# One ScalarE operation for both 16-bit planes of a tile, in place of one on ScalarE and one on GpSimd

## The chip, the cores and the metric

The kernel runs on one core of one Trainium2 chip. The metric is the device time of one execution in microseconds, from the first to the last instruction and a little around them; lower is better. The engines are named as the profile names them: PE is TensorE (PEld its weight loads), DVE is VectorE, ACT is ScalarE, POOL is GpSimd and SP is SyncE, which here only issues DMAs.

## The reference

One block of a network on 1024 tokens of width 512: a layer norm, then a Mamba-2 mixer and a mixture-of-experts linear layer on its output, both added to the input. What matters here is the mixer:

```python
xn = _layernorm(x)
proj = einsum('bsd,ed->bse', xn, in_proj_w)          # gate | hBC | dt
hBC = silu(causal_conv4(hBC) + conv_b)               # depthwise, 4 taps
hs, Bm, Cm = split(hBC)                              # hs: 128 heads of 64
...                                                  # chunks of 128 tokens:
Y = Y_diag + Y_off + hs * D                          # scan with decays exp(cumsum(dt * A))
g = Y * silu(gate)
out = groupwise_rms_norm(g) * norm_w
return x + einsum('bsi,oi->bso', out, out_proj_w) + moe(xn)
```

All of it is in fp32. The kernel keeps that precision by splitting operands of matmuls into a high and a low part (names that end in H and L), so a product takes three matmuls.

## The kernel before

The mixer is cut into 16 slices of 8 heads and each slice into 8 chunks of 128 tokens. The main loop runs over the 128 pairs, here called steps m = 0 to 127, with s = m // 8 the slice and c = m % 8 the chunk. Every engine has its own program, an order written out by hand, and engines meet only at semaphores. Each engine takes its instructions strictly in order.

In a step TensorE does, in this order: blocks of the B/C tile (L324, L325), a part of the input projection of a later slice (L257 to L259), the two state products (L446 to L458), 32 small products of the decay matrix EM (L466), the output projection of the step before (L476 to L483), the gate product of the next step (L334 to L341), and last the transposes of the gated result yb (L491). The result yb is made by VectorE: L1045 adds the parts of Y in PSUM and L1048 multiplies by the gate. So L1048 of step m must end before L491 of step m can start.

The tiles that feed the slices are [128 channels, 1024 tokens]. Such a tile passes through: projection on TensorE (into two PSUM banks), `act_tap` on ScalarE (L516, first tap of the convolution), `dve_conv` on VectorE (L784, three more taps, one after the other), `act_tanh` on ScalarE (L534), `dve_silu` on VectorE (L813). A tile of hs is wanted in transposed form (tokens on partitions). It is therefore seen as 16-bit numbers, its low and its high halves are copied into two planes of one buffer `low_high`, stored to DRAM (`sp_halves`), and read back by a 16-bit transposing DMA (`sp_turned`) as chunks `HT`. The high plane is copied by ScalarE (`act_high_half`, L543) and the low plane by GpSimd (`pool_low_half`, L1092), each with a semaphore of its own. The store waits for both, and so does `act_tap` before it writes over a tile's buffer two tiles later. Both copies wait until the store of the tile before has landed.

There are 60 such tiles. The list `slot_halves` puts their copies into the steps with m mod 16 = 1, 3, 5, 6, 7, 9, 11 and 15 as far as the first tile slices and the last ones go (the first slice has one more in step 4; the last copy is in step 117). The order of ScalarE's work in a step is: rounding of new gate weights to GH where a slice ends (L548), eight ReLUs for the decays (L579), `act_tap`, exponential of the decays (L584), rounding of the state S and of dxh to their high parts SH and DH (L592, L598), eviction or scaling of an output (L737 or L742), square of yb (L749), tanh of the gate (L752), rounding of the transposed result (L757), small roundings for B and C (L565, L566), output weights where a slice begins (L765, L767), **the copy of the high plane (L543)**, rounding of the next projection weights (L503), `act_tanh` (L534). In a slice's first step `act_tap` comes before the ReLUs.

The order of GpSimd's work in a step is: scaled tile xch of the next step (L1103), the sum of yb and dhs (L1173), low parts of the state operands (L1112, L1115), scaling of S (L1118), dhs (L1125), in odd slices the norm's small operations (L1185 to L1189), once a slice a low part of weights (L1192), **the copy of the low plane (L1092)**, low part of the next projection weights (L1078), in odd slices a sum of outputs (L1206). VectorE multiplies the decays by Gt into EM (L854); in a step that finishes a tile that comes after L1048, otherwise before L1045.

Of the kernel before, what the change touches and what calls it, by code (L numbers as in the profile page):

```python
# [6 lines left out]
def mamba_moe_block_kernel(nc, x, wa, wg, wo, wdt, cw, cbias, nw, dtb, alog, dvec, wbase, wrt, wla, wlb,  # L7
# [97 lines left out]
    with ctx:  # L105
# [3 lines left out]
        def sem(name):  # L109
            return ctx.enter_context(nc.semaphore(name))  # L110
# [87 lines left out]
        al_in = [sem(f"al_in{i}") for i in range(2)]  # L198
        half_st = [sem(f"half_st{i}") for i in range(4)]
        ht_in = [sem(f"ht_in{i}") for i in range(2)]  # L200
        s_hi, s_lo = sem("high_half"), sem("low_half")
        ring_hi, ring_lo = sem("ring_hi"), sem("ring_lo")
        s_xt, s_xh, s_xl, s_bst, s_mv, s_var, s_rs, s_nmr, s_xnd, s_xna = (
            sem(n) for n in ("xt", "xh_", "xl_", "bst", "mv_", "var", "rs", "nmr_", "xnd", "xna"))
# [70 lines left out]
        def turned_no(i):  # L275
            t = ctiles[i]
            return 4 * (t[1] - 1) + t[2] if t[0] == "H" and t[1] else None
# [227 lines left out]
        def act_tap(i):  # L505
            n, t = chan(ctiles[i]), ctiles[i]
            se.wait_ge(s_a, i + 1)
            se.wait_ge(s_half, 2)
            if t[0] == "H" and t[1] and turned_no(i) > 1:
                se.wait_ge(s_hi, turned_no(i) - 1)  # L510
                se.wait_ge(s_lo, turned_no(i) - 1)
            elif t[0] != "H" and t[1] > 0:
                se.wait_ge(s_bg, 4 * t[1])
                se.wait_ge(s_ch, 4 * t[1])
                se.wait_ge(s_cl, 4 * t[1])
            se.activation(tile_out(i), pair("A", i), ACT.Identity, bias=cbt[:, n:n + 1], scale=cwt[:, n, 3:4]).then_inc(s_tap, 1)  # L516
# [16 lines left out]
                se.wait_ge(s_x, i)  # L533
            se.activation(th[:, :], tile_out(i), ACT.Tanh).then_inc(s_th, 1)  # L534

        def act_high_half(i):
            n = turned_no(i)
            if n is None:
                return
            se.wait_ge(s_x, i + 1)  # L540
            if n:
                se.wait_ge(half_st[(n - 1) % 4], 16 * ((n - 1) // 4 + 1))
            se.activation(low_high[:, 1, :], halves_of(i)[:, 1, :], ACT.Copy).then_inc(s_hi, 1)  # L543

        def act_gate_hi(s, ks=range(4)):
            se.wait_ge(ts_in, 16 * (2 + 2 * s))
# [53 lines left out]
        def act_program():  # L600
# [111 lines left out]
            for m in range(M + 1):  # L712
                s, c = divmod(m, 8)
                pm, pc, ps = m - 1, (m - 1) % 8, (m - 1) // 8
                done = [k // 2 for k in slot_halves[m + 1] if k % 2] if m < M else []
                new_gate = c == 7 and s + 1 < NS
                if new_gate:
                    se.wait_ge(s_gt, m + 1)
                    act_gate_hi(s + 1, (0, 1, 3))
                if m < M and c == 0:  # L720
                    for i in done:
                        act_tap(i)
                if m + 1 < M:
                    act_relus(m + 1)
                if m < M and c:
                    for i in done:
                        act_tap(i)
                if m + 1 < M:
                    act_exp(m + 1)
                    if new_gate:  # L730
                        act_gate_hi(s + 1, (2,))
                    act_state_hi(m + 1)
                if m and ps % 2 == 0:
                    se.wait_ge(s_o, m)
                    if pm >= 2:
                        se.wait_ge(acc_st[(pm - 2) % 8], 16 * ((pm - 2) // 8 + 2))
                    se.activation(pl[pc % 2][:, :], bank("O", pm), ACT.Copy).then_inc(s_pl, 1)  # L737
                if m and ps % 2:
                    n_ = ngc(pm)
                    se.wait_ge(pl_in[pc % 2], 16 * ((n_ + 1) // 2))  # L740
                    se.wait_ge(s_rst, n_)
                    se.activation(pl[pc % 2][:, :], pl[pc % 2][:, :], ACT.Copy, scale=rst[:, pc, 1:2]).then_inc(s_plr, 1)  # L742
                if m < M:
                    se.wait_ge(s_g, m + 1)
                    if s >= 2:
                        se.wait_ge(s_rst, 8 * ((s - 2) // 2) + c + 1)
                    if m:
                        se.wait_ge(s_sq, m)
                    se.activation(sq[:, :], yb[:, :], ACT.Square, accum_out=sqs[:, s % 2, c:c + 1]).then_inc(s_sq, 1)  # L749
                if m + 1 < M:  # L750
                    se.wait_ge(s_gt, m + 2)
                    se.activation(tg[:, :], bank("GT", m + 1), ACT.Tanh, scale=0.5).then_inc(s_tg, 1)  # L752
                if m < M:
                    se.wait_ge(s_gtr, m + 1)
                    if m:
                        se.wait_ge(s_o, m)
                    se.activation(gTh[:, :, :], bank("GTr", m).rearrange("p (k t) -> p k t", k=4), ACT.Copy).then_inc(s_gth, 1)  # L757
                    if m + 2 < M:
                        act_front(m + 2)
                    if c == 0:  # L760
                        se.wait_ge(s_ts3, s + 1)
                        se.wait_ge(ts_in, 16 * (3 + 2 * s))
                        if m:
                            se.wait_ge(s_o, m)
                        se.activation(OH[:, 3, :], TS[:, 3, :], ACT.Copy).then_inc(s_oh, 1)  # L765
                        for j in range(3):
                            se.activation(OH[:, j, :], TS[:, j, :], ACT.Copy, scale=nwt[:, 4 * s + j:4 * s + j + 1]).then_inc(s_oh, 1)  # L767
                    for k in slot_halves[m]:
                        if k % 2:
                            act_high_half(k // 2)  # L770
                    for i in done:
                        act_ring(i + 4)
                        act_tanh(i)
# [308 lines left out]
                pe_.wait_ge(s_gh, 4 * n + (4 if n > 1 and k == 2 else k + 1))  # L1082
                pe_.tensor_tensor(GL[:, k, :], TS[:, k, :], as_f(GH[:, k, :]), ALU.subtract).then_inc(s_gl, 1)

        def pool_low_half(i):
            n = turned_no(i)
            if n is None:
                return
            pe_.wait_ge(s_x, i + 1)
            if n:  # L1090
                pe_.wait_ge(half_st[(n - 1) % 4], 16 * ((n - 1) // 4 + 1))
            pe_.tensor_copy(low_high[:, 0, :], halves_of(i)[:, 0, :]).then_inc(s_lo, 1)  # L1092

        def pool_scaled(m):
            s, c = divmod(m, 8)
            if s:
# [30 lines left out]
        def pool_program():  # L1127
# [30 lines left out]
            for m in range(M + 1):  # L1158
# [4 lines left out]
                if m < M:  # L1163
                    if c == 0:
                        pe_.wait_ge(ts_in, 16 * (3 + 2 * s))
                        pe_.tensor_tensor(TS[:, 3, :], TS[:, 3, :], nwt[:, 4 * s + 3:4 * s + 4].broadcast_to([128, 512]),
                                          ALU.mult).then_inc(s_ts3, 1)
                    if new_gate:
                        pool_gate_lo(2 + s, (0, 1))
                    if c:  # L1170
                        pe_.wait_ge(s_t1, n0(m))
                        pe_.wait_ge(s_dhs, m + 1)
                        pe_.tensor_tensor(yb[:, :], yb[:, :], dhs[:, :], ALU.add).then_inc(s_tp, 1)  # L1173
                    if new_gate:
                        pool_gate_lo(2 + s, (2,))
                        pool_scaled(m + 1)
                    if m + 1 < M:
                        pool_front(m + 1)
                    if s % 2:
                        n_ = ngc(m)  # L1180
                        pe_.wait_ge(s_sq, m + 1)
                        if n_ > 8:
                            pe_.wait_ge(s_alo, n_ - 8)
                            pe_.wait_ge(s_plr, n_ - 8)
                        pe_.tensor_tensor(rst[:, c, 0:1], sqs[:, 0, c:c + 1], sqs[:, 1, c:c + 1], ALU.add).then_inc(s_v, 1)  # L1185
                        pe_.wait_ge(s_v, 2 * n_ - 1)
                        pe_.tensor_scalar(rst[:, c, 0:1], rst[:, c, 0:1], 1.0 / 1024, 4 * EPS, ALU.mult, ALU.add).then_inc(s_v, 1)
                        pe_.wait_ge(s_v, 2 * n_)
                        pe_.tensor_tensor(rst[:, c, 1:2], rst[:, c, 0:1], mhalf[:, :], ALU.pow).then_inc(s_rst, 1)  # L1189
                    if c == 0:  # L1190
                        pe_.wait_ge(s_oh, 4 * s + 1)
                        pe_.tensor_tensor(OL[:, 3, :], TS[:, 3, :], as_f(OH[:, 3, :]), ALU.subtract).then_inc(s_olp, 1)  # L1192
                    for k in slot_halves[m]:
                        if k % 2:
                            pool_low_half(k // 2)
                    for k in slot_halves[m + 1]:
                        if k % 2:
                            pool_ring(k // 2 + 4)
# [24 lines left out]
        def sp_halves(i):  # L1223
            n = turned_no(i)
            if n is None:
                return
            sp.wait_ge(s_hi, n + 1)
            sp.wait_ge(s_lo, n + 1)
            sp.dma_start(half_d[(n // 4 + 1) % 2, n % 4], low_high).then_inc(half_st[n % 4], 16)

        def sp_turned(m):
# [157 lines left out]
```

## Time and profile before

| | before |
|---|---|
| median of 3 runs | 1659.66 us (1659.27 to 1663.36) |
| the profiled execution: its time | 1658.31 us |
| the profiled execution: its span, first to last instruction | 1656.8 us |
| mean granted TensorE clock | 0.998 |
| L543 on ACT, all 60 | 63.8 us busy |
| L1092 on POOL, all 60 | 65.9 us busy |

The profile is of one execution. "Busy" is time in which an engine has an instruction at work. The time in brackets behind an instruction is how long its engine stood idle just before it, and for which instruction it waited. A share of busy time is a mean over the whole kernel. Matmuls overlap and their ends are modelled, so two matmuls in a row are best compared by their starts.

### The profile page before, as it was taken

The numbers are of one execution on the slowest core, as the hardware profiler recorded it, in microseconds if no ns is written. First come the engines' busy times: TensorE is split into PE (matmuls) and PEld (weight loads), VectorE is DVE, ScalarE is ACT, GpSimd is POOL, SyncE is SP. The second block draws the span as 40 slices with busy tenths as digits, with TensorE's granted clock in tenths as the row PEclk, the third lists the DMA queues.
The fourth block names the chain that finished last, engine by engine and source line by source line (L and its number), as shares of the span: only waits on it lengthen the run. The fifth ranks groups of instructions, "written<-read, shape, count | busy, mean of one in ns | idle before, by whom it ended". The sixth has DMA issues, their size and how long they took to land.

```text
span 1656.8 us, 31784 instructions
## 1 busy us (share of the span) xinstructions
PE 1618.2 (98%) x10792; PEld 1301.6 (79%) x10792; DVE 1356.9 (82%) x1667; ACT 1236.1 (75%) x2633; POOL 1346.9 (81%) x1246
## 2 busy tenths in 40 slices
PE   7999999999999999999999999999999999999998
PEld 6778878878787877878778787877778787787766
DVE  5878788887879878798888888888788887889775
ACT  5277787777877777777877778787786868778775
POOL 3148689886999779897798969988798977989798
PEclk9999999999999999999999999999999999999999
DMA  3253367554665646664665536655465465655464
GB/s 128 71 190 109 109 178 201 172 169 109 197 185 159 168 143 193 154 183 117 183 205 166 160 115 191 193 161 165 143 191 173 148 162 161 196 163 169 125 175 130
DMA packets 232527, 265.46 MB, mean 160 GB/s; under 512 B 156072, under 2 KB 157616, under 8 KB 228144
## 3 DMA queue, kind: packets, MB, share of 16 engines
q1 hardware_dynamic: 232368, 263.45, 53.7%
q8 instruction: 87, 1.43, 0.4%
q14 instruction: 72, 0.59, 0.1%
HBM read 162.20 MB, written 69.73 MB: 140 GB/s over the span
## 4 chain that ended last, share of the span: by engine, by line
PE 60%; POOL 16%; DVE 8%; ACT 8%; issue 7%; DMA 0%; ACTq 0%; POOLq 0%; DVEq 0%; SPq 0%
PE P L257 8%; PE P L259 7%; PE P L258 7%; PE P L466 5%; PE P L476 5%; PE P L341 4%; PE P L477 4%; PE P L334 4%; PE P L483 4%; PE P L335 4%; ACT P L579 3%; PE P L491 2%; DVE hsX L784 2%; POOL xch L1103 2%; POOL al L1206 2%
## 5 line engine op out<-in xcount | busy, mean ns | idle before, releaser
L579 ACT ACTIVATE P<-AB,SC 128x128 f32<-128x128 f32 x1016 | 305.7, 363 | 0.0
L257 PE MATMUL P<-xh,AH 128*128 128x512 f32 x656 | 268.0, 409 | 2.0 <-DVE xl L885 2.0
L784 DVE SCALAR_TENSOR_TENSOR hsX<-P,cwt,hsX 128x1023 f32<-128x1023 f32 x189 | 241.9, 1280 | 25.5 <-ACT hsX L516 21.1
L259 PE MATMUL P<-xh,AL 128*128 128x512 f32 x656 | 257.4, 392 | 0.0
L258 PE MATMUL P<-xl,AH 128*128 128x512 f32 x656 | 255.8, 390 | 0.0
L749 ACT ACTIVATE sq<-yb 128x512 bf16<-128x512 f32 x128 | 80.7, 631 | 214.0 <-DVE yb L1048 214.0
L1078 POOL TENSOR_TENSOR AL<-AR,AH 128x512 fp32r<-128x512 f32 x82 | 117.2, 1429 | 134.1 <-ACT AH L503 134.1
L476 PE MATMUL P<-OH,gTh 128*128 128x512 f32 x512 | 215.0, 420 | 2.3 <-issue 1.5
L334 PE MATMUL P<-GH,xh 128*128 128x512 f32 x512 | 200.9, 392 | 0.2 <-ACT GH L548 0.2
L854 DVE TENSOR_TENSOR EM<-P,Gt 128x1024 f32<-128x1024 f32 x127 | 154.6, 1218 | 56.5 <-ACT P L584 29.5
L335 PE MATMUL P<-GH,xl 128*128 128x512 f32 x512 | 200.5, 392 | 0.0
L477 PE MATMUL P<-OH,gTl 128*128 128x512 f32 x512 | 200.4, 392 | 0.0
L1173 POOL TENSOR_TENSOR yb<-yb,dhs 128x512 f32<-128x512 f32 x112 | 145.6, 1300 | 55.3 <-DVE yb L1017 55.2
L466 PEld LDWEIGHTS P<-xch,EM 128*64 128x64 f32 x4096 | 130.6, 138 | 47.3 <-issue 44.7
L1125 POOL TENSOR_TENSOR dhs<-hsX,Dbc 128x512 f32<-128x512 f32 x128 | 136.8, 1069 | 35.2 <-DVE P L1045 35.2
L1112 POOL TENSOR_TENSOR SL<-S,SH 128x512 fp32r<-128x512 f32 x112 | 145.0, 1295 | 23.7 <-ACT SH L592 23.3
L1115 POOL TENSOR_TENSOR DL<-dxh,DH 128x512 fp32r<-128x512 f32 x112 | 159.3, 1422 | 0.4 <-ACT DH L598 0.4
L1103 POOL TENSOR_TENSOR xch<-hsX,SC 128x512 f32<-128x512 f32 x128 | 156.0, 1218 | 2.1 <-ACT hsX L558 2.1
L1017 DVE TENSOR_TENSOR yb<-P,SC 128x512 f32<-128x512 f32 x112 | 77.1, 689 | 91.5 <-PE P L449 76.3
L466 PE MATMUL P<-xch,EM 128*64 128x64 f32 x4096 | 148.3, 226 | 2.2 <-ACT hsX L558 2.2
L259 PEld LDWEIGHTS P<-xh,AL 128*128 128x128 f32 x656 | 123.1, 188 | 27.8
L483 PE MATMUL P<-OL,gTh 128*128 128x512 f32 x512 | 139.4, 391 | 4.7 <-DVE OL L807 4.7
(213 smaller groups left out, 4144.8 us busy)
## 6 DMA issues: line engine op xcount, KB each, us to landing
AB<-acr_d SPq DMA_DIRECT2D x128, 512.0 KB, 5.0
half_d<-hsX SPq DMA_DIRECT2D x60, 512.0 KB, 3.5
AR<-in_wa SPq DMA_DIRECT2D x80, 256.0 KB, 2.9
TS<-in_wg SPq DMA_DIRECT2D x16, 1024.0 KB, 6.7
TS<-in_wo SPq DMA_DIRECT2D x16, 1024.0 KB, 6.4
part_d<-pl SPq DMA_DIRECT2D x64, 256.0 KB, 3.1
pl<-part_d SPq DMA_DIRECT2D x64, 256.0 KB, 2.6
al<-acc_d SPq DMA_DIRECT2D x64, 256.0 KB, 3.0
```

Source lines behind the costliest of these rows:

```text
L257: te.matmul(o, ah_, bh_, start=(first and i == 0), stop=False)
L258: te.matmul(o, ah_, bl_, start=False, stop=False)
L259: r = te.matmul(o, al_, bh_, start=False, stop=(last and i == n - 1))
L334: te.matmul(o, xh[:, k, tok(c)], GH[:, k, :], start=n_ == 0, stop=False)
L335: te.matmul(o, xl[:, k, tok(c)], GH[:, k, :], start=False, stop=False)
L466: r = te.matmul(o[f:f + 64, h * 64:(h + 1) * 64], EM[m % 2][:, at_ + f:at_ + f + 64], xch[m % 2][:, h * 64:(h + 1) * 64], start=True, stop ...
L476: te.matmul(o, gTh[:, k, :], OH[:, k, :], start=k == 0, stop=False)
L477: te.matmul(o, gTl[:, k, :], OH[:, k, :], start=False, stop=False)
L483: r = te.matmul(o, gTh[:, k, :], OL[:, k, :], start=False, stop=k == 2)
L579: r = se.activation(decays(m)[:, h, :], AB[m % 2][:, h, :], ACT.Relu, bias=SC[s % 2][:, c, 3, h:h + 1], scale=-1.0)
L784: ve.scalar_tensor_tensor(out=o[:, d:T], in0=raw[:, 0:T - d], scalar=cwt[:, n, 3 - d:4 - d], in1=o[:, d:T], op0=ALU.mult, op1=ALU.add).the ...
L1103: pe_.tensor_tensor(h8(xch[m % 2][:, :]), h8(HT[m % 2]), bc(SC[s % 2][:, c, 0, :]), ALU.mult).then_inc(s_xch, 1)
```

## The change

ScalarE copies both planes in one operation of [128, 2, 1024] 16-bit numbers; GpSimd's copy and its semaphore go, and with them the second wait of the store and of `act_tap`. The place of the copy in ScalarE's order stays as it was.

```diff
-        s_hi, s_lo = sem("high_half"), sem("low_half")
+        s_hi = sem("halves")
...
             if t[0] == "H" and t[1] and turned_no(i) > 1:
                 se.wait_ge(s_hi, turned_no(i) - 1)
-                se.wait_ge(s_lo, turned_no(i) - 1)
...
-        def act_high_half(i):
+        def act_halves(i):
             n = turned_no(i)
             if n is None:
                 return
             se.wait_ge(s_x, i + 1)
             if n:
                 se.wait_ge(half_st[(n - 1) % 4], 16 * ((n - 1) // 4 + 1))
-            se.activation(low_high[:, 1, :], halves_of(i)[:, 1, :], ACT.Copy).then_inc(s_hi, 1)
+            se.activation(low_high, halves_of(i), ACT.Copy).then_inc(s_hi, 1)
...
-        def pool_low_half(i):
-            n = turned_no(i)
-            if n is None:
-                return
-            pe_.wait_ge(s_x, i + 1)
-            if n:
-                pe_.wait_ge(half_st[(n - 1) % 4], 16 * ((n - 1) // 4 + 1))
-            pe_.tensor_copy(low_high[:, 0, :], halves_of(i)[:, 0, :]).then_inc(s_lo, 1)
-
...
-                    for k in slot_halves[m]:
-                        if k % 2:
-                            pool_low_half(k // 2)
...
             sp.wait_ge(s_hi, n + 1)
-            sp.wait_ge(s_lo, n + 1)
             sp.dma_start(half_d[(n // 4 + 1) % 2, n % 4], low_high).then_inc(half_st[n % 4], 16)
```

## Rows read from the trace of the kernel before

**Rows 1.** The page: engines' busy time, and the chain that ended last by engine.
```profile
PE 1618.2 (98%) x10792; PEld 1301.6 (79%) x10792; DVE 1356.9 (82%) x1667; ACT 1236.1 (75%) x2633; POOL 1346.9 (81%) x1246
...
PE 60%; POOL 16%; DVE 8%; ACT 8%; issue 7%; DMA 0%; ACTq 0%; POOLq 0%; DVEq 0%; SPq 0%
```
**Rows 2.** Waits, 121 to 1600 us: who waited for whom, us in total, times, longest.
```profile
ACT sq L749 <- DVE yb L1048: 196.7, 114, 3.9
...
DVE P L1045 <- POOL yb L1173: 7.0, 21, 0.5
```
**Rows 3.** Groups by form: line, tiles, shapes, count | busy us, mean ns | idle.
```profile
L1092 POOL COPY hsX<-hsX 128x1024 uint16<-128x1024 uint16 x60 | 65.9, 1098 | 0.0
L543 ACT ACTIVATE hsX<-hsX 128x1024 uint16<-128x1024 uint16 x60 | 63.8, 1064 | 2.5 <-DVE hsX L813 2.5
L503 ACT ACTIVATE AH<-AR 128x512 fp32r<-128x512 f32 x82 | 52.0, 634 | 0.0
```
**Rows 4.** Timeline, step 65 into 66: start, length, engine, line [idle before, releaser].
```profile
928.80 1.07 ACT L543 ACTIVATE hsX<-hsX 128x1024 uint16<-128x1024 uint16 x1
...
932.09 1.20 ACT L516 ACTIVATE hsX<-P,cbt,cwt 128x1024 f32<-128x1024 f32 x1
...
933.32 3.92 DVE L784 SCALAR_TENSOR_TENSOR hsX<-P,cwt,hsX 128x1023 f32<-128x1023 f32 x3 [0.54 <-ACT hsX L516]
...
937.73 1.07 PE L341 MATMUL P<-GL,xh 128*128 128x512 f32 x4
...
937.88 0.69 DVE L1048 TENSOR_TENSOR yb<-P,tg 128x512 f32<-128x512 f32 x1
...
938.72 0.63 PE L491 MATMUL P<-ident,yb 128*128 128x128 f32 x4
```
**Rows 5.** Timeline, step 67 into 68.
```profile
956.45 3.92 DVE L784 SCALAR_TENSOR_TENSOR hsX<-P,cwt,hsX 128x1023 f32<-128x1023 f32 x3 [0.26 <-ACT hsX L516]
...
961.00 0.69 DVE L1048 TENSOR_TENSOR yb<-P,tg 128x512 f32<-128x512 f32 x1
...
961.14 1.07 PE L341 MATMUL P<-GL,xh 128*128 128x512 f32 x4
...
962.05 0.60 PE L491 MATMUL P<-ident,yb 128*128 128x128 f32 x4
```
**Rows 6.** Timeline, step 70 into 71.
```profile
999.46 1.22 DVE L854 TENSOR_TENSOR EM<-P,Gt 128x1024 f32<-128x1024 f32 x1 [2.56 <-ACT P L584]
...
1002.16 0.63 PE L491 MATMUL P<-ident,yb 128*128 128x128 f32 x4 [0.33 <-DVE yb L1048]
```
**Rows 7.** Timeline, step 73 into 74.
```profile
1030.82 3.92 DVE L784 SCALAR_TENSOR_TENSOR hsX<-P,cwt,hsX 128x1023 f32<-128x1023 f32 x3 [0.89 <-ACT hsX L516]
...
1036.21 0.63 PE L491 MATMUL P<-ident,yb 128*128 128x128 f32 x4 [0.36 <-DVE yb L1048]
```
**Rows 8.** Timeline: the first tap in steps 63 and 71, and in step 69 with L784.
```profile
906.52 1.21 ACT L516 ACTIVATE hsX<-P,cbt,cwt 128x1024 f32<-128x1024 f32 x1 [1.08 <-PE P L259]
...
1005.58 1.21 ACT L516 ACTIVATE hsX<-P,cbt,cwt 128x1024 f32<-128x1024 f32 x1 [0.89 <-PE P L259]
...
982.87 1.21 ACT L516 ACTIVATE hsX<-P,cbt,cwt 128x1024 f32<-128x1024 f32 x1
...
984.84 1.27 DVE L784 SCALAR_TENSOR_TENSOR hsX<-P,cwt,hsX 128x1023 f32<-128x1023 f32 x1
```
**Rows 9.** Timeline, step 63 to the end of step 64 and yb of step 65.
```profile
908.25 1.04 POOL L1092 COPY hsX<-hsX 128x1024 uint16<-128x1024 uint16 x1
...
919.16 1.73 POOL L1078 TENSOR_TENSOR AL<-AR,AH 128x512 fp32r<-128x512 f32 x1
...
925.38 1.07 PE L341 MATMUL P<-GL,xh 128*128 128x512 f32 x4
...
925.41 0.70 DVE L1045 TENSOR_TENSOR P<-P,yb 128x512 f32<-128x512 f32 x1 [0.53 <-POOL yb L1173]
...
926.14 0.69 DVE L1048 TENSOR_TENSOR yb<-P,tg 128x512 f32<-128x512 f32 x1
...
926.98 0.63 PE L491 MATMUL P<-ident,yb 128*128 128x128 f32 x4 [0.52 <-DVE yb L1048]
```

More of the change, by code:

```diff
@@ L769, in act_program @@
                         if k % 2:
-                            act_high_half(k // 2)
+                            act_halves(k // 2)
                     for i in done:
```

## The prediction

> **What bounds the kernel now.** I read the page first. TensorE is busy 98% of the span, GpSimd 81% and ScalarE 75%; the chain that ended last lies 60% on TensorE, 16% on GpSimd and 8% on ScalarE [rows 1]. So TensorE is nearly full, and what counts is only what makes it wait, or stops doing so. Next the view of waits: ScalarE stands idle 196.7 us before its square of yb, once in nearly every step [rows 2]. That looks like ample room for more work on ScalarE. But this room lies behind the tap and the exponential, not in front of them, so I went to the timeline and followed each of the steps that hold a copy to the next L491. The kernel repeats itself every 16 steps, so one step of a kind stands for all.
>
> In that timeline the reader is to look at one distance. From the start of TensorE's four L341 matmuls to the start of L491 it is 0.91 us when nothing is waited for (961.14 to 962.05, [rows 5]). In step 65 it is 1.60 us (925.38 to 926.98, [rows 9]), in step 66 0.99 us (937.73 to 938.72, [rows 4]); the rest over 0.91 is a wait for yb. L491 starts 0.15 us after L1048 ends when it waits (926.14 + 0.69 = 926.83, then 926.98). By that measure the end of step 66 has no room at all, step 68 has 962.05 - (961.00 + 0.69 + 0.15) = 0.21 us, and steps 71 and 74 already wait, for the row of each has idle time put down to yb [rows 6, 7].
>
> **What the change costs on ScalarE.** One operation now covers 2048 numbers a partition and not 1024. The trace has none of that size. From 512 to 1024 numbers a Copy goes from 634 to 1064 ns [rows 3], so 1024 more cost 2 x 0.43 = 0.86 us and the new operation should take 1.92 us. Bounds: not over a whole further pass of 1.06 us, and from below nothing, if a pair of 16-bit numbers went through as one word. For that the 16-bit row would have to be faster per element than the fp32 one, and by this slope it isn't: I take 0.86 us and keep 0 and 1.06 for the rivals. It comes 60 times, 51 us of ScalarE's time. Behind it in ScalarE's order stand the rounding L503, tanh L534, the ReLUs, the tap and the exponential.
>
> Step 65 into 66, eight times in the kernel (m = 1, 17, ... 113): from the copy at 928.80 to the tap at 932.09 ScalarE has no idle time, VectorE's convolution then waits 0.54 us for that tap, runs without a break into L1045 and L1048, and TensorE waits for yb [rows 4]. Each link is tight, so all 0.86 us reach TensorE: 8 x 0.86 = 6.9 us.
>
> Step 67 into 68, six times and once more in step 115: the convolution waits 0.26 us for the tap, and yb has 0.21 us of room [rows 5]: 0.65 us each. Step 117, where the exponential takes the tap's place, I count the same: 8 x 0.65 = 5.2 us.
>
> Step 70 into 71, seven times: no tap, but L854 waits 2.56 us for the exponential and L1045 and L1048 follow at once; L491 waits already [rows 6]: 7 x 0.86 = 6.0 us.
>
> Step 73 into 74, seven times: L784 waits 0.89 us for the tap, and L491 waits already [rows 7]: 7 x 0.86 = 6.0 us.
>
> The other copies are covered. In steps 63 and 71 the tap waits 1.08 and 0.89 us for TensorE's projection [rows 8], more than 0.86 (without that cover they would cost up to 14 x 0.86 = 12 us). In step 69 the tap ends at 984.08, but L784 starts only at 984.84, since VectorE is at other work [rows 8]; step 75 and the first slice's steps 3 to 5 go the same way. Sum of the losses: 6.9 + 5.2 + 6.0 + 6.0 = 24.1 us.
>
> **What it gives on GpSimd.** Sixty copies of 1.10 us, 65.9 us in all [rows 3], leave the engine. That shows only where VectorE waits for GpSimd's sum L1173 and TensorE for VectorE. Up to 1600 us such waits are 7.0 us over 21 times [rows 2], and no copy stands behind that time. GpSimd works without a pause from the copy in step 63 (908.25) over L1078 (919.16) to that sum; then L1045 has waited 0.53 us and L491 0.69 [rows 9]. With 1.04 us less in front, VectorE's own work becomes the limit: 0.53 us, seven times, 3.7 us. In the other 14 cases (steps 9 and 15 of each 16) GpSimd's run starts from a wait for ScalarE that comes later than the last copy, so nothing moves. Bounds: 0 and the whole 7.0 us.
>
> **Semaphores and DMAs.** The store of the planes now waits for one event. In step 65 the low plane was the later one, in step 70 the high plane; the store comes sooner in the one and 0.86 us later in the other, stands behind other issues in SyncE's queue anyway, and its tile is read back at least a step later. The removed wait of the tap was for copies two tiles back. I cost both at nothing; if the read-back came late, GpSimd's L1103 would show a wait for a DMA.
>
> Sum: 24.1 - 3.7 = +20.4 us. On the profiled execution's 1658.31 us that is 1678.7; the median of the runs is 1.35 us above that execution, so 1680.1, say 1680 us.
>
> **A rule weighed.** Rows say that GpSimd is busier than ScalarE, 1346.9 against 1236.1 us [rows 1], and that after the change it would be 1281 against 1288. The Trainium skill, "Perfetto Trace Analysis", Optimizing GPSIMD Operations, says to prefer other engines to GpSimd where one can. By that rule the move is a gain, at most the 7.0 us above, and the sum would be 1653 instead of 1680. The same page's section on Scalar/DVE operations speaks against this change: where such an engine isn't full but makes others wait, it advises to break instructions up so that work ends sooner, and here one is made longer. The rows side with the second: ScalarE is idle, and late.
>
> **The rivals.** *GpSimd's relief wins* (faster). It is the busiest helper and 16% of the chain [rows 1]. If ScalarE's 0.86 us vanished in its idle time before the square and all GpSimd waits went, 1659.7 - 7.0 = 1652.7 us. Against it: the idle time comes after the tap. It decides if the added time is under 0.2 us per copy (22 to 30 places against 7 us). Chance 0.04; the rule above points here.
>
> *The 16-bit pairs go at one word each*: the new operation takes 1.06 us like the old, nothing is lost and 3.7 us are won, 1656 us, within the noise. Chance 0.06.
>
> *Part of the delay hides.* Each wait of TensorE also lets GpSimd and VectorE catch up. If that swallowed the cases of step 68 and of step 74, 20.4 - 5.2 - 6.0 = 9.2 us stay: 1669 us. For it: the room in step 68 is there already. Against: steps 71 and 74 wait on a chain that starts from TensorE itself. Chance 0.13.
>
> *A dear operation.* A whole further pass, 1.06 us, also outgrows the cover of 0.89 us in step 71: 22 x 1.06 + 8 x 0.85 + 7 x 0.17 - 3.7 = 27.6 us: 1687 us. Chance 0.09.
>
> **How the numbers follow.** The forecast has the remaining 0.68, with a range of its own of 1673 to 1685 us (0.80 to 0.95 us per copy, a gain on GpSimd of 0 to 7). The range for 8 in 10 reaches down to the partly hidden case and up to the dear one: 1666 to 1688. About 0.3% (5 us) is what a measurement of this kernel can tell from no change. Slower by more than that: 0.68 + 0.13 + 0.09 = 0.90; the same: 0.06; faster: 0.04.
>
> **What the profile after would show.** Right: L543 at about 1.92 us; the waits of L784 for L516 after steps 65, 67 and 73 grown by 0.86; L341 to L491 at about 1.85 us in step 66 (was 0.99), 1.56 in 68 (0.91) and 1.07 in 65 (1.60); the idle time before L491 at about 1.2 us in steps 71 and 74 (0.33 and 0.36); the DVE wait for L1173 down from 7.0 to some 3.3 us. Wrong: an operation near 1.06 us, these distances as before, or a GpSimd wait for a DMA before L1103.

## The result, and the profile after

| | before | after |
|---|---|---|
| median | 1661.51 us (4 runs, 1659.27 to 1666.63) | 1679.32 us (4 runs, 1678.59 to 1681.76) |
| the profiled execution: time, span | 1658.31, 1656.8 us | 1681.76, 1680.5 us |

The change makes the kernel slower by 17.8 us, a ratio of 1.0109 [1.0087, 1.0132]. The forecast was 1680. The profiled execution of after is the longest of its four, and that of before is shorter than any of its own four, so the two traces stand 23.5 us apart; the section on why the prediction was right takes that apart.

**The page of after**: busy time by engine, the chain that ended last by engine, and the copy in the groups by form. They answer to [rows 1] and [rows 3]; line numbers under L503 are unchanged, L543 is now L542, and below that most moved by one to ten lines (L784 is L783, L1045 is L1044, L1048 is L1047, L1173 is L1163).

```profile
PE 1621.0 (96%) x10792; PEld 1299.7 (77%) x10792; DVE 1361.0 (81%) x1667; ACT 1285.1 (76%) x2633; POOL 1291.3 (77%) x1186
...
PE 53%; ACT 13%; POOL 13%; DVE 10%; issue 9%; DMA 1%; ACTq 0%; SPq 0%; DVEq 0%; POOLq 0%
```
```profile
L542 ACT ACTIVATE hsX<-hsX 128x2048 uint16<-128x2048 uint16 x60 | 115.1, 1918 | 2.5 <-DVE hsX L812 2.5
```

The new operation takes 1918 ns, the 1.92 us of the forecast. ScalarE and GpSimd are now busy for nearly the same time (1285 and 1291 us; VectorE, at 1361, is busier than both), TensorE's share has fallen from 98% to 96%, and in the chain ScalarE has grown from 8% to 13%. So the busy shares look better balanced than before, and the kernel is slower.

**The waits of after**, 121 to 1600 us (who waited for whom: us in total, times, longest), answering to [rows 2]:

```profile
ACT sq L748 <- DVE yb L1047: 204.5, 112, 3.9
...
DVE hsX L783 <- ACT hsX L515: 31.2, 22, 1.8
...
PE P L491 <- DVE yb L1047: 26.3, 38, 1.8
...
DVE P L1044 <- POOL yb L1163: 8.2, 21, 1.8
...
ACT hsX L515 <- PE P L259: 6.8, 14, 0.8
```

ScalarE's idle time in front of the square did not shrink, it grew (196.7 to 204.5 us): the room that looked free was never used. In the same view of before, the convolution's wait for the first tap was 12.5 us and TensorE's wait for yb 9.0 us in 23 places; they are now 31.2 and 26.3. The tap's own wait for TensorE's projection was 20.3 and is 6.8: nearly all of that is the cover of steps 63 and 71 and their like (1.08 us before and 0.20 after in step 64, 0.89 and none in step 72), eaten up at no cost.

**The timeline of after, step 65 into 66**, answering to [rows 4]:

```profile
939.17 1.92 ACT L542 ACTIVATE hsX<-hsX 128x2048 uint16<-128x2048 uint16 x1
...
944.54 3.92 DVE L783 SCALAR_TENSOR_TENSOR hsX<-P,cwt,hsX 128x1023 f32<-128x1023 f32 x3 [1.39 <-ACT hsX L515]
...
948.10 1.07 PE L341 MATMUL P<-GL,xh 128*128 128x512 f32 x4
...
949.94 0.63 PE L491 MATMUL P<-ident,yb 128*128 128x128 f32 x4 [0.77 <-DVE yb L1047]
```

The convolution's wait went from 0.54 to 1.39 us, and L341 to L491 from 0.99 to 1.84 us. **Step 67 into 68** answers to [rows 5], and **steps 70 into 71 and 73 into 74** to [rows 6, 7]:

```profile
968.50 3.92 DVE L783 SCALAR_TENSOR_TENSOR hsX<-P,cwt,hsX 128x1023 f32<-128x1023 f32 x3 [1.11 <-ACT hsX L515]
...
972.34 1.07 PE L341 MATMUL P<-GL,xh 128*128 128x512 f32 x4
...
973.90 0.63 PE L491 MATMUL P<-ident,yb 128*128 128x128 f32 x4 [0.50 <-DVE yb L1047]
```
```profile
1012.70 0.50 PE L334 MATMUL P<-GH,xh 128*128 128x512 f32 x1 [0.60 <-ACT GH L547]
...
1014.91 0.63 PE L491 MATMUL P<-ident,yb 128*128 128x128 f32 x4 [0.32 <-DVE yb L1047]
...
1044.43 3.91 DVE L783 SCALAR_TENSOR_TENSOR hsX<-P,cwt,hsX 128x1023 f32<-128x1023 f32 x3 [1.75 <-ACT hsX L515]
...
1049.82 0.63 PE L491 MATMUL P<-ident,yb 128*128 128x128 f32 x4 [1.21 <-DVE yb L1047]
```

Step 68 shows 1.56 us from L341 to L491, step 74 an idle time of 1.21 us before L491, both as forecast. Step 71 does not: before L491 it shows 0.32 us as before, and the delay stands 2 us earlier, as a new wait of 0.60 us for the last quarter of the rounding of GH (L547), which ScalarE does behind the exponential. The step is longer all the same (next table).

**Step 64 to the end of step 65**, answering to [rows 9]:

```profile
927.66 1.29 POOL L1182 TENSOR_TENSOR OL<-TS,OH 128x512 fp32r<-128x512 f32 x1
...
929.43 0.68 DVE L841 TENSOR_TENSOR dxh<-hsX,SC 128x512 f32<-128x512 f32 x1
929.52 1.73 POOL L1077 TENSOR_TENSOR AL<-AR,AH 128x512 fp32r<-128x512 f32 x1 [0.56 <-ACT AH L503]
...
935.74 1.07 PE L341 MATMUL P<-GL,xh 128*128 128x512 f32 x4
935.76 0.70 DVE L1044 TENSOR_TENSOR P<-P,yb 128x512 f32<-128x512 f32 x1 [0.53 <-POOL yb L1163]
...
937.33 0.63 PE L491 MATMUL P<-ident,yb 128*128 128x128 f32 x4 [0.53 <-DVE yb L1047]
```

Here nothing looks as forecast: VectorE still waits 0.53 us for GpSimd's sum, and L341 to L491 is still 1.59 us. And yet the step is 0.8 us shorter. To see that, take the distance from the start of the first L491 matmul of one step to that of the next. In this table each number is the median over the six cycles of 16 steps from 17 to 112, against before; a step that isn't named differs by at most 0.02 us.

| step mod 16 | before | after |
|---|---|---|
| 1 | 13.21 | −0.79 |
| 2 | 11.74 | +0.86 |
| 4 | 11.65 | +0.65 |
| 5 | 14.37 | +0.04 |
| 7 | 11.39 | +0.85 |
| 10 | 11.87 | +0.84 |

It matters that matmuls are compared here and not the weight loads of L491. A load starts 0.23 us before its matmul where nothing is waited for, and 0.03 us before it where yb is waited for. Between loads step 1 would read 13.41 us, and step 4 would seem to grow by 0.85 and step 5 to give 0.16 back. The lengths of 12.6, 12.9 and 13.8 us for step 1 in an expectation further down are distances of that kind; by matmuls they are 12.4, 12.7 and 13.6 us.

### The profile page after: what moved, and what is told of

It is laid out like the page before. It is cut to its first block, busy times and chain, and to the rows that moved or that the text cites. A ratio compares the mean times of both kernels' runs of the same rounds, so it can differ in the third digit from the quotient of the medians.

```text
span 1680.5 us, 31547 instructions
## 1 busy us (share of the span) xinstructions
PE 1621.0 (96%) x10792; PEld 1299.7 (77%) x10792; DVE 1361.0 (81%) x1667; ACT 1285.1 (76%) x2633; POOL 1291.3 (77%) x1186
## 4 chain that ended last, share of the span: by engine, by line
PE 53%; ACT 13%; POOL 13%; DVE 10%; issue 9%; DMA 1%; ACTq 0%; SPq 0%; DVEq 0%; POOLq 0%
PE P L257 7%; PE P L259 7%; PE P L258 7%; ACT P L578 5%; PE P L466 4%; PE P L476 4%; DVE hsX L783 4%; PE P L341 3%; PE P L477 3%; PE P L483 3%; PE P L335 3%; PE P L334 3%; ACT hsX L542 3%; PE P L491 2%; DVE P L1044 2%
## 5 line engine op out<-in xcount | busy, mean ns | idle before, releaser
L783 DVE SCALAR_TENSOR_TENSOR hsX<-P,cwt,hsX 128x1023 f32<-128x1023 f32 x189 | 241.9, 1280 | 44.3 <-ACT hsX L515 39.8
L1077 POOL TENSOR_TENSOR AL<-AR,AH 128x512 fp32r<-128x512 f32 x82 | 113.7, 1387 | 184.3 <-ACT AH L503 184.2
L334 PE MATMUL P<-GH,xh 128*128 128x512 f32 x512 | 201.0, 393 | 4.4 <-ACT GH L547 4.4
L1163 POOL TENSOR_TENSOR yb<-yb,dhs 128x512 f32<-128x512 f32 x112 | 145.7, 1301 | 55.5 <-DVE yb L1016 55.5
L1093 POOL TENSOR_TENSOR xch<-hsX,SC 128x512 f32<-128x512 f32 x128 | 166.2, 1299 | 1.8 <-ACT hsX L557 1.8
L257 PEld LDWEIGHTS P<-xh,AH 128*128 128x128 f32 x656 | 123.5, 188 | 25.6 <-DVE xl L884 2.7
L258 PEld LDWEIGHTS P<-xl,AH 128*128 128x128 f32 x656 | 123.7, 189 | 22.6
```

The costliest lines, as they stand in the source:

```text
L257: te.matmul(o, ah_, bh_, start=(first and i == 0), stop=False)
L258: te.matmul(o, ah_, bl_, start=False, stop=False)
L334: te.matmul(o, xh[:, k, tok(c)], GH[:, k, :], start=n_ == 0, stop=False)
L783: ve.scalar_tensor_tensor(out=o[:, d:T], in0=raw[:, 0:T - d], scalar=cwt[:, n, 3 - d:4 - d], in1=o[:, d:T], op0=ALU.mult, op1=ALU.add).the ...
L1093: pe_.tensor_tensor(h8(xch[m % 2][:, :]), h8(HT[m % 2]), bc(SC[s % 2][:, c, 0, :]), ALU.mult).then_inc(s_xch, 1)
```

## The experiments

All come from the kernel before. Their own medians stand beside before's of the same chip, since before's varies from chip to chip: 1661.24 us (11 runs) for the first four, 1667.95 (14 runs) for the next four, 1661.96 (15 runs) for the last three. On the second chip before ran at granted clocks down to 0.993 and took 1663.58 to 1677.4 us, while the four changed kernels ran at 0.996 and more; their ratios therefore flatter them by some 0.4%, and the step lengths say more.

### Cost alone

ScalarE writes both planes; GpSimd makes its copy as before, but into a scratch tile.

```diff
-            se.activation(low_high[:, 1, :], halves_of(i)[:, 1, :], ACT.Copy).then_inc(s_hi, 1)
+            se.activation(low_high, halves_of(i), ACT.Copy).then_inc(s_hi, 1)
...
-            pe_.tensor_copy(low_high[:, 0, :], halves_of(i)[:, 0, :]).then_inc(s_lo, 1)
+            pe_.tensor_copy(scr[:, :], halves_of(i)[:, 0, :]).then_inc(s_lo, 1)
```

> ScalarE copies both planes in one operation as in the changed kernel, and GpSimd still makes its copy of the low plane in its old place, but into a scratch buffer that nothing reads; the output is the reference's. Theory A (two separate terms: a late ScalarE costs about 24 us at four kinds of steps, GpSimd's relief gives about 5 us): 24 us slower than the kernel before, ratio 1.0145, 4 to 6 us more than the changed kernel; steps 2, 4, 7 and 10 of each 16 longer by 0.86, 0.65, 0.86 and 0.86 us and step 1 as before. Rival B (GpSimd's relief gives nothing, the whole difference is ScalarE's): the same as the changed kernel, +18 us, ratio 1.011. Rival C (the time comes from the later store and the read-back, not from ScalarE's order): also +18, with step 1 shorter as in the changed kernel.

Measured: 1685.16 us, ratio 1.0144 [1.0127, 1.0161], +23.9 us. Steps 2, 7 and 10 grow by 0.85 to 0.86 us and step 4 by 0.65, each as expected; step 1 stays (+0.03). This is the cost of the longer operation: the working had 24.1.

### Relief alone

ScalarE writes the high plane as before; GpSimd's copy and the two waits for it are left out, so the low plane is never written.

```diff
-            pe_.tensor_copy(low_high[:, 0, :], halves_of(i)[:, 0, :]).then_inc(s_lo, 1)
```

> GpSimd's copy is left out and ScalarE copies the high plane alone as before, so the low plane that is stored is never written: the transposed tiles are wrong in their low bits. Theory A: 0.82 us less in step 1 of each 16, seven times, 5.7 us faster, ratio 0.9965, all other steps unchanged, and VectorE's dxh in that step at 0.68 us in place of 1.78. Rival B (no gain from GpSimd): ratio 1.000, step 1 unchanged. If GpSimd were a bound elsewhere too: up to 7 us or more.

Measured: 1655.84 us, ratio 0.9968 [0.9956, 0.9979], −5.4 us. Step 1 falls by 0.80 us in the median (0.55 in the mean), every other step is as before. The two halves add up: 23.9 − 5.4 = 18.5 us, against 17.8 of the whole. In its timeline, step 64 into 65, the same picture stands as in after:

```profile
919.22 0.68 DVE L863 TENSOR_TENSOR dxh<-hsX,SC 128x512 f32<-128x512 f32 x1
919.31 1.73 POOL L1099 TENSOR_TENSOR AL<-AR,AH 128x512 fp32r<-128x512 f32 x1 [0.57 <-ACT AH L514]
...
925.56 0.70 DVE L1066 TENSOR_TENSOR P<-P,yb 128x512 f32<-128x512 f32 x1 [0.53 <-POOL yb L1195]
```

In the kernel with the cost alone they stand as in before, with VectorE's product dxh more than twice as long:

```profile
930.69 1.76 POOL L1216 TENSOR_TENSOR OL<-TS,OH 128x512 fp32r<-128x512 f32 x1
931.21 1.78 DVE L865 TENSOR_TENSOR dxh<-hsX,SC 128x512 f32<-128x512 f32 x1
932.41 1.73 POOL L1101 TENSOR_TENSOR AL<-AR,AH 128x512 fp32r<-128x512 f32 x1
```

### The covered copies alone, and the uncovered ones

`copy_mode(m)` says who makes the copies of step m: "act" is the change, "split" is before.

```diff
+    def copy_mode(m):
+        return "split" if m % 16 in (1, 3, 6, 9) or m > 112 else "act"
```

> The change is made only for the copies whose delay should be covered: steps with m mod 16 = 5, 7, 11 and 15, and 4 and 5 of the first slice; in steps 1, 3, 6 and 9 and after step 112 both engines copy as before. Theory A: no loss, the whole gain of step 15's copy, so 5.7 us faster, ratio 0.9965. If the cover is thinner than read from the trace (a tap wait of 0.89 us in step 71 against 0.86 added): up to 6 us of loss against it, ratio 1.000. Rival (every copy on ScalarE costs its share, 0.3 us on average): 8 us slower.

Measured: 1656.11 us, ratio 0.9958 [0.9933, 0.9983], −5.1 us: the same gain in step 1 (−0.79 in the median), and no other step of the 16 grows. Steps 49 and 97 themselves are 0.58 and 0.27 us longer than before, since GpSimd there waited 1.50 and 1.13 us for a load of output weights; more on that below. And the complement:

```diff
+        return "act" if m % 16 in (1, 3, 6, 9) or m > 112 else "split"
```

> The complement of the run on covered steps: the change only for copies in steps with m mod 16 = 1, 3, 6 and 9 and after step 112. Theory A: the whole loss and no gain, 24 us slower than the kernel before, ratio 1.0145, and this difference and that of the covered steps add up to that of the changed kernel. Rival (the cost is spread over all 60 copies): 9 to 10 us slower, ratio 1.006.

Measured: 1684.82 us, ratio 1.0141 [1.012, 1.0162], +23.6 us, steps 2, 7 and 10 grown by 0.85 to 0.86, step 4 by 0.64, step 1 by 0.03. So all of the loss comes from the copies in four steps of 16 (and three late ones), and all of the gain from the others.

### Step 15 alone

```diff
+        return "act" if m % 16 == 15 else "split"
```

> Only the copies of the steps with m mod 16 = 15 are made as in the changed kernel (seven of 60); all others as before. Theory A: the whole gain of GpSimd's relief comes from these seven copies, through the run of GpSimd that starts behind them: 0.80 us less in step 1 of each 16, so up to 5.6 us faster, ratio 0.9966, and every other step unchanged. Rival (relief anywhere helps): a share of it, 7/60, 0.7 us, ratio 0.9996.

Measured: 1655.61 us (1652.96 to 1657.56), ratio 0.9916 [0.9882, 0.9949]. The ratio is one of the flattered ones; in the traces, from the second L491 to the last, it is 3.9 us less than before, where GpSimd's relief alone gives 4.2. Step 1 falls by 0.80 us in the median and no other step of the 16 changes. The seven copies that GpSimd makes in steps 15, 31, ... 111 are the whole of the gain; the other 53 that left GpSimd brought nothing.

### Two operations in place of one

```diff
-                se.activation(low_high, halves_of(i), ACT.Copy).then_inc(s_hi, 1)
+                se.activation(low_high[:, 0, :], halves_of(i)[:, 0, :], ACT.Copy)
+                se.activation(low_high[:, 1, :], halves_of(i)[:, 1, :], ACT.Copy).then_inc(s_hi, 1)
```

(This excerpt is against the changed kernel.)

> As the changed kernel, but ScalarE makes the two planes in two operations of 1024 numbers, one after the other, and GpSimd none. The operations start 0.95 us apart, so a copy costs 0.95 us more than before and not 0.85. Theory A (time goes as what ScalarE adds, at 29 uncovered places): 3 us slower than the changed kernel, 0.1 us in each of steps 2, 4, 7 and 10; ratio to the kernel before 1.013; step 8 may grow a little, since the cover of 0.89 us is used up. Rival (a fixed loss per copy, not its length): as the changed kernel, 1.011.

Measured: 1683.15 us, ratio 1.0082 [1.0055, 1.011] (flattered too), 3.8 us above the change on another chip. Steps 2, 7 and 10 grow by 0.94 to 0.95 us in place of 0.85, and step 4 by 0.74 in place of 0.65; step 8 stays. Over the 30 uncovered places (the expectation says 29) that makes 2.9 us more in the trace than in that of after, the 3 of theory A. The groups by form have the first at 1064 ns and the second at 1061, and they start 0.95 us apart. One operation saves 0.09 us a tile over two; that the second plane goes to ScalarE at all costs 0.85.

### The copy later in ScalarE's order

If the place in the order and not the amount of work is what costs, moving the copy behind the tap and the exponential of the next step should free the path. Here it moves behind the roundings of SH and DH, in steps 1, 9 and (but for the first slice) 3 of each 16; "split" stays after step 116.

```diff
                    act_state_hi(m + 1)
+                if m:
+                    for k in slot_halves[m - 1]:
+                        if k % 2:
+                            act_copy(k // 2, m - 1, True)
...
+        return "split" if m > 116 else "late" if m % 16 in (1, 3, 9) and m != 3 else "act"
```

> As the changed kernel, but the copies of steps with m mod 16 = 1, 3 and 9 (not step 3) stand behind the ReLUs, the tap, the exponential and the two roundings of the next step, in front of the wait for yb; after step 116 both engines copy as before. Theory A (it is the place in ScalarE's order that costs): steps 2, 4 and 10 lose nothing and even a bit of the old wait goes (0.1 and 0.5 us), step 7 keeps its 0.85 and step 1 its gain of 0.8: per 16 steps 0.5 to 0.6 us less than the kernel before, some 2 to 4 us faster in all, ratio 0.998. Rival B (ScalarE's total work costs): as the changed kernel, 1.011. Rival C: the store, issued up to 7 us later, makes the read-back late, and GpSimd waits for a DMA before the scaled tile: slower than the kernel before.

Measured: 1656.26 us, ratio 0.9924 [0.9897, 0.9952]. Step 2 goes from +0.86 to −0.08, step 4 from +0.65 to 0.00, step 10 from +0.84 to −0.53: the 0.1 and 0.5 us of theory A. Step 7, not touched, stays at +0.85. But for one copy ScalarE does the same work as after the change. The ratio again flatters: 1656.26 us is 4 to 6 us below the medians of before on the other chips (1660.26 to 1661.96 us). Rival C is there in part: GpSimd's scaled tile waits 4.1 us in all for the read-back, in steps 84, 115 and 117, and VectorE's dxh 2.1 us in two; yet the kernel is faster.

### And step 6's copy on GpSimd

In step 70 nothing comes in ScalarE's order behind which the copy could hide, and GpSimd has idle time there. So GpSimd makes both planes in that one step of 16.

```diff
+                pe_.tensor_copy(low_high, halves_of(i)).then_inc(s_hi, 1)
...
+        return "split" if m > 116 else "late" if m % 16 in (1, 3, 9) and m != 3 else "pool" if m % 16 == 6 else "act"
```

> As the run with the copy later, and in step 6 of each 16 GpSimd makes both planes in one operation of 2048 numbers, in a place where it stood idle for 2.1 us, so ScalarE has no copy in front of the exponential of step 7. Theory A: step 7 falls under the kernel before by the wait that TensorE has there, 0.7 us, and with the others 2.0 us per 16 steps: 12 to 15 us faster than the kernel before, ratio 0.992. Rival: GpSimd's longer copy delays L1078 and the low parts of the gate weights, and step 7 stays where it was or grows: ratio 0.998 or more.

Measured: 1646.71 us (1644.86 to 1647.64), ratio 0.9862 [0.9838, 0.9887]. Step 7 goes from +0.85 to −0.75, the wait that was to go. The copies in the groups by form, and then the timeline of step 66 (`dve_conv` is L806 here) in this kernel:

```profile
L561 ACT ACTIVATE hsX<-hsX 128x2048 uint16<-128x2048 uint16 x52 | 99.5, 1913 | 0.0
...
L1115 POOL COPY hsX<-hsX 128x2048 uint16<-128x2048 uint16 x7 | 13.2, 1889 | 0.0
```
```profile
924.87 3.91 DVE L806 SCALAR_TENSOR_TENSOR hsX<-P,cwt,hsX 128x1023 f32<-128x1023 f32 x3
...
926.40 1.90 ACT L561 ACTIVATE hsX<-hsX 128x2048 uint16<-128x2048 uint16 x1
```

The convolution starts with no idle time before it, and the copy runs while it works, where ScalarE used to wait for yb: the wait before the square has fallen to 178.8 us, from 204.5 after the change.

### Before again, the placed copies again, and the output weights

The kernel before, unchanged, is a control for how far its steps vary. Beside it the placed copies run again, and once more with the load of the output weights cut in two, so that its last quarter, which GpSimd's scaling (L1166 in before) takes, starts earlier.

> The kernel before itself, unchanged, with a profile of its own: a control for the last group, where it ran 6 us longer than elsewhere. If that was the state of the chip in that hour: ratio 1.000 and the step lengths of the first trace. If the kernel before has a slow form of its own (step 1 of some slices 1.3 us longer), its profile or the spread of its times shows it.

> The run with placed copies once more, for a ratio beside an undisturbed kernel before. Theory A: 1646 to 1648 us, 13 to 14 us faster, ratio 0.9915. If the ratio of 0.986 was real: 0.986 again.

```diff
-                        sp.wait_ge(s_gl, ngl(s + 2))
                        sp.wait_ge(s_gl3, s + 1)
-                        sp.dma_start(TS[:, :, :], wo[s + 1]).then_inc(ts_in, 16)
+                        sp.dma_start(TS[:, 3, :], wo[s + 1][:, 3, :]).then_inc(x_in[0], 16)
+                        sp.wait_ge(s_gl, ngl(s + 2))
+                        sp.dma_start(TS[:, 0:3, :], wo[s + 1][:, 0:3, :]).then_inc(ts_in, 16)
```

> As the run with placed copies, and the load of the output weights is cut in two: the quarter that GpSimd scales first (L1166) is loaded as soon as its part of the buffer is free, with an event of its own, and the other three quarters as before. Theory D (in the slices where step 1 gave no gain, GpSimd stood idle for this load, which lands late): no idle time before L1166 in slices 6 and 12, step 1 at 12.6 us in steps 49 and 97 too, where it was 12.9 and 13.8, and 1 to 3 us faster than with placed copies alone. Rival (the two slow steps come from the order in which VectorE and GpSimd get at the buffers and not from the load): they stay at 12.9 and 13.8, and the time stays. A cost of its own may come from one more issue in SyncE's queue.

| | us | ratio to before |
|---|---|---|
| before again (10 runs) | 1660.26 (1658.52 to 1667.65) | 0.999 [0.9976, 1.0004] |
| placed again (5 runs) | 1646.93 (1643.32 to 1647.55) | 0.991 [0.9896, 0.9923] |
| placed, weights cut (5 runs) | 1647.03 (1645.09 to 1647.61) | 0.9913 [0.9899, 0.9926] |

The control's step 1 (the second of the 128) is 14.24 us, where the first profile of before had 12.43: the product dxh took 1.76 us in place of 0.68. Step 121 is 0.55 longer too. In after both are longer by the same, 1.78 and 0.55. So these 2.3 us belong to the single execution, not to the change. All other steps of the control agree with the first profile within 0.05 us. The row of the control, and the one of after:

```profile
130.43 1.76 DVE L842 TENSOR_TENSOR dxh<-hsX,SC 128x512 f32<-128x512 f32 x1
```
```profile
130.46 1.76 DVE L841 TENSOR_TENSOR dxh<-hsX,SC 128x512 f32<-128x512 f32 x1
```

The placed kernel beats before on an undisturbed chip too, by 0.9%, as theory A had it; the 0.986 came from the long times of before on the other chip. In after (first row, step 96 into 97) and in the placed kernel (second, a line of its waits, 121 to 1600 us) GpSimd at times waits for the output weights:

```profile
1319.04 1.04 POOL L1156 TENSOR_TENSOR TS<-TS,nwt 128x512 f32<-128x512 f32 x1 [1.42 <-DMA TS<-in_wo]
```
```profile
POOL TS L1189 <- DMA TS<-in_wo: 8.7, 7, 1.9
```

With the load cut, no slice has that wait any more, and step 49, at 13.50 us in the placed kernel's profile, is 12.41, as is step 97. So theory D has the cause of the two slow steps right, and its 1 to 3 us did not come: the medians are the same. From the first L491 to the last the trace has 1509.4 us in place of 1512.0, but 1.8 of these 2.6 us are step 1, long in the one execution and short in the other as in the two of before; from the second L491 on it is 0.8 us. The first L491 starts at 126.79 us and not at 123.87. In the other traces it lies between 122.3 and 126.4 us without any cut, so one profile doesn't say whether the two loads delay the start; that stays open.

## Why the prediction was right, and where it was not

**The operation's duration** was right: 1.92 us from a slope of 0.43 us per 512 numbers, 1918 ns measured. The rival of pairs at one word each is out, the dear one too: one more plane moves a step by 0.85 us.

**The losses** were right, in place and in size. In the profile of after, step 2 of each 16 lost 8 x 0.85 = 6.8 us (6.9 forecast), step 4 and its two late kin 8 x 0.65 = 5.2 (5.2), steps 7 and 10 lost 6.0 and 5.9 (6.0 and 6.0). Another 0.6 us was lost where the working had nothing: 0.04 in each step 5 and 0.2 behind each of the two late copies, in steps 117 and 119. Together 24.5 against 24.1. The room of 0.21 us in step 68 did absorb, just where the working had it. The covered copies were costless, as the run of those alone shows. That part of the delay hides, the rival with 0.13, is refuted.

**The sign for step 71** was wrong, not its price. The working followed the exponential into L854 and expected all of the delay before L491. The row of after has it at L334: the rounding of GH's last quarter comes behind the exponential on ScalarE too, and its wait (0.2 us in one place in before) is met first.

**The gain on GpSimd** was mis-sized, and its mechanism half wrong. The step of the working that failed is "With 1.04 us less in front, VectorE's own work becomes the limit: 0.53 us, seven times, 3.7 us". It was 0.80 us, seven times, less what one execution's load of weights takes back. These are the rows of before that the working did not show:

```profile
916.56 1.49 DVE L807 SCALAR_TENSOR_TENSOR OL<-TS,nwt,OH 128x512 fp32r<-128x512 f32 x1
...
917.44 1.76 POOL L1192 TENSOR_TENSOR OL<-TS,OH 128x512 fp32r<-128x512 f32 x1
...
917.97 1.78 DVE L842 TENSOR_TENSOR dxh<-hsX,SC 128x512 f32<-128x512 f32 x1
```

Three things happen in its place, counted from the end of yb in step 64 (913.10 in before, 924.28 in after, 11.18 us later):

- GpSimd comes to its low part of the output weights, OL, 0.96 us earlier (917.44 in before, 927.66 − 11.18 = 916.48) and ends it before VectorE starts dxh. So dxh takes 0.68 us and not 1.78, while VectorE's own OL just before it takes 1.77 and not 1.49, and VectorE is 0.82 us earlier at the end of dxh. It did not become the limit, since it was held up by the same engine that it later waits for; the working counted the 1.78 us as VectorE's own.
- GpSimd then has to wait 0.56 us for ScalarE's AH, which is the new limit: AL starts 0.82 us earlier, not 1.04. (In the relief alone, with ScalarE's copies as before, it is 0.57.)
- Both engines move by the same amount, so the wait between them stays at 0.53 us. That is why the sign I named (1.07 us from L341 to L491, the wait for L1173 down to 3.3 us) did not show, and the gain did.

That GpSimd's earliness is what counts, and not dxh's own length, the traces show where GpSimd lost part of it again to a late load of output weights. In five such steps dxh took 1.78 to 1.80 us and yet the step was 0.1 to 0.7 us shorter than before, with the wait for GpSimd's sum at 0.53 us. Step 49 of the run with step 15 alone is the clearest. GpSimd waited 0.23 us for the load, the step is 12.51 us (13.21 before), and VectorE made the time up in OL, at 0.76 us in place of 1.49:

```profile
714.81 1.04 POOL L1189 TENSOR_TENSOR TS<-TS,nwt 128x512 f32<-128x512 f32 x1 [0.23 <-DMA TS<-in_wo]
...
720.59 0.76 DVE L829 SCALAR_TENSOR_TENSOR OL<-TS,nwt,OH 128x512 fp32r<-128x512 f32 x1
...
721.27 1.79 DVE L864 TENSOR_TENSOR dxh<-hsX,SC 128x512 f32<-128x512 f32 x1
...
728.72 0.70 DVE L1067 TENSOR_TENSOR P<-P,yb 128x512 f32<-128x512 f32 x1 [0.54 <-POOL yb L1196]
```

In all 13 steps with such a wait, over eight traces, GpSimd's wait for the load and the gain of the step add up to 0.86 to 0.94 us: a wait of 0.23 leaves 0.70, one of 0.80 leaves 0.11, and one of 1.42 (step 97 of after) makes the step 0.50 us longer. Without such a wait the gain is 0.8, held there by the wait for AH. So OL and dxh on VectorE stretch or shrink with where GpSimd stands, and the wait for the sum stays (it is longer, 1.78 us, only where GpSimd had waited 1.13 us or more). The Trainium skill, "SBUF — State Buffer", Terms, says that VectorE and GpSimd arbitrate for a port pair which one holds for its whole instruction while the other is blocked. The rows agree: in before OL runs to 919.20, dxh ends 0.55 us later at 919.75, and GpSimd's AL, started at 919.16, takes 1.73 us where its median over the kernel is 1.30.

**The sum.** Losses 24.5, gain 7 x 0.80 = 5.6, less 1.3 for step 97, where GpSimd waited 1.42 us for the output weights and dxh took 1.53 us: 4.3. That leaves 20.2 us in the profiled pair, against 20.4 forecast, and so close a match is luck: the gain was taken 1.9 us too small, the losses 0.4 too small, and one execution's wait for a load took 1.3 us back. The 2.3 us of steps 1 and 121 come on top, which before shows in one execution and not in another: 22.5 from the first L491 to the last. The start and the tail (−0.4 and +1.6 us) make it the 23.6 of the spans. The tail behind the last L491 is 8.0 us in six of the 13 traces and 9.5 to 9.6 in the other seven; what decides between them stays open. By medians it is 17.8 us, and 18.5 by the two halves on one chip.

**Stores and events** at nothing: no wait of GpSimd's L1093 for a DMA in after, as the forecast wanted. It does show up in the placed kernel, 4.2 us over four times, and 2.5 us over three before VectorE's dxh, where the copies come later.

**Slips of the working** that moved little. The busiest helper is VectorE (1356.9 us) and not GpSimd (1346.9), by its own rows. GpSimd's busy time after the change was to be 1281 us and is 1291.3, since its scaled tiles (L1103) take 10.3 us more in all. And the narrow range of 1673 to 1685 us doesn't follow from its terms: 0.80 us a copy with a gain of 7.0 gives 1675, and 0.95 with no gain 1686.5.

**The rule weighed.** Preferring another engine to GpSimd paid in seven copies of 60. Moving the work costs 24 us where the copy was put. With the copy behind the exponential and, once in 16 steps, whole on GpSimd, the kernel is 14 us faster than before, and by the traces some 4 of these come from GpSimd's relief and 10 from the place.

## What to carry to other kernels

Idle time of an in-order engine is room only for work that comes after what others wait for: 196.7 us of it hid none of the uncovered copies, while the same operations behind the exponential cost nothing and even took old waits away. So before moving work to a less busy engine, follow the first instruction queued behind it to the engine that is the bound, and look for a place in the order where that instruction is already through. When relief on one engine is priced by who becomes the next limit, check whether that one's own durations are stretched by the engine relieved, for then both move and the wait between them stays.

## What the runs showed of the hardware

- The same product of VectorE (128x512, both inputs from SBUF) took 0.68, 1.53 or 1.78 us, depending on what GpSimd did beside it; in step 1 it took 0.68 us in one execution of before and 1.76 in another.
- Between 1024 and 2048 16-bit numbers ScalarE's copy grows by 0.85 us (1064 to 1918 ns), GpSimd's from 1.04 us where nothing stretched it (mean 1.10) to 1.89: the two engines are nearly equal at it.
- Two copies one behind the other on ScalarE start 0.95 us apart though each shows 1.06, so a second operation costs 0.09 us over a longer one.
